# Joining block inverses in four steps in place of nine, in a macaron layer with gated delta-rule attention

## The chip, the core and the metric

The kernel runs on one core of a Trainium2 chip. The metric is the device time of one execution in microseconds (us), the median of several runs. The core has TensorE (PE in the profile; its weight loads are listed apart as PEld), VectorE (DVE), ScalarE (ACT), GpSimd (POOL), and a queue that issues DMA transfers (SP). Each engine works through its own list of instructions in order, and they wait for one another through semaphores.

## What is computed

The input is `x`, 8 batches of 512 rows of 128 numbers, in float32. For each batch:

```python
x = x + 0.5 * ffn(layernorm(x))          # "f1": 128 -> 512 -> 512 -> 512 -> 128, ternary weights
x = x + attn(layernorm(x))               # below
x = x + 0.5 * ffn(layernorm(x))          # "f2", the same weights

def attn(x):                             # 8 heads of 128
    n = layernorm(x) * ln1_w + ln1_b
    q, k, v = l2norm(silu(n @ Wq)), l2norm(silu(n @ Wk)), silu(n @ Wv)
    beta, alpha = sigmoid(n @ Wb), sigmoid(n @ Wa)
    # over time: S = alpha (I - beta k k^T) S + beta v k^T ;  o = S^T q
    x = x + o @ Wo
    return x + gelu(layernorm2(x) @ W1 + b1) @ W2 + b2
```

The recurrence over time is computed in chunks of 128 rows. Within a chunk it needs the inverse of a unit triangular 128x128 matrix for each of 4 chunks x 8 heads = 32 units.

## The kernel before

**The inverse.** Each unit's matrix is cut into blocks of 32. GpSimd inverts the four diagonal blocks of all 32 units together by elimination (`invert`), and DMAs (`back`) put the block inverses into the tile `R` (straight) and their transposed partners into `TB`. TensorE then joins neighbouring blocks, first two of 32 into 64 (for the pair of blocks 0, 1 and the pair 2, 3), then two of 64 into 128. A join is two products: the off-diagonal block times one inverse (kinds `p32` and `p64`; the result goes, negated, to `TB`), then times the other inverse (kinds `r32` and `r64`; the result goes to `R`). For the first pair alone a third product (`t32`) gives the same joined block transposed, which the 64-wide join needs in `TB`. Each matmul is 32x32x32 or 64x64x64 and works on one unit, in the part of the array that its rows and output partitions give.

**The nine steps** (`STEPS`, L272). A step has two sides; side 0 writes bank 6, side 1 bank 7, and the matmuls of the sides alternate: 16 on each side in steps 0 to 4 (32 wide), 8 on each in steps 5 to 8 (64 wide), 224 matmuls in all. A matmul is listed in the trace as two records. After a step VectorE copies bank 6 out (`joined`, L904) and ScalarE bank 7 (L1065), one instruction each, and `join_waits` (L1688) holds TensorE before the next step until both are done. The kinds by step are p32|p32, p32|p32, r32|r32, r32|t32, t32|r32, p64|p64, p64|r64, p64|r64, r64|r64.

**Where the steps run.** The loop over time `t` runs three things of different batches one after the other on TensorE: `SP(t-1, t, t+1)`, the scan over the four chunks of batch s = t-1 mixed with the projections of batch p = t and the start of the first FFN of batch t+1; `F1(t+1)`, the rest of that first FFN; and `F2(t-1)`, the second FFN of batch t-1 in 20 slots. A slot is two matmuls of 512 columns (four records), in the last four slots four matmuls of 128 columns. Steps 0 to 6 of batch t run behind slots 6, 8, 10, 12, 14, 16 and 18 of `F2` (`JOIN_SLOTS`). Steps 7 and 8 (`AHEAD` = 7) run in `SP_first` of the batch, between `solve`, `proj`, `update` and `output`. The last batch has its steps 0 to 6 behind slots 10, 12, 14, 16, 17, 18 and 19 (`LATE_SLOTS`). Batch 0 has no FFN beside it: `lone_join` (L1727) runs steps 0 to 6 one after another, two `proj` between them, with a small matmul (`hold`) ahead of each.

**What stands around the change.** VectorE's order in the second FFN of batch t-1 is joined(t,0), joined(t,1), `LN_F1`, joined(t,2), joined(t,3), then the gates of the next batch with the rest of the copies between. In `SP_first` TensorE's order is solve (two), proj 2 and 3, step 7, update 0, proj 0, update 1, proj 1, output (two), step 8, proj 4 and 5, attend. ScalarE copies the solved rows and the outputs out and applies silu to each projection; a projection's bank (4 or 5) is free again after that silu. VectorE copies the new state, takes `squares` of the keys, and after GpSimd's power normalizes and turns the keys (`unit_k`); then SP stores them (`k_store`) and loads them back turned into `KT` (`k_load`), for `keys_keys(p, 0)` in the next part of the scan.

## Time and profile before

| | us |
|---|---|
| median of 3 runs | 1491.02 |
| lowest and highest | 1490.46, 1491.98 |
| the profiled execution's own time | 1489.32 |
| its span in the trace | 1487.6 |
| TensorE matmul busy | 1418.9 (95%) |
| VectorE, ScalarE, GpSimd busy | 820.9, 668.6, 564.9 |
| mean granted TensorE clock | 0.982 of full |

The steady part repeats with a period of 173.3 us per batch, batches 1 to 6. The rows of the section below are lines of the profile: the busy times, the windows table, the chain that ended last, the timeline of one engine, and the answers for one line of the kernel. In a timeline row the numbers are the start and the duration in us, then the engine, the line, the operation, the result and its inputs, the tile shape, the output shape and the count of records that the row merges; brackets hold the idle time before it and what ended it.

### The profile page before, as it was taken

The page shows a single profiled execution, that of the slowest core. Times are in us where ns is not written, and L with a number is a line of the kernel's source. Part 1 is how long each engine was busy: PE and PEld are TensorE (multiplying, and loading weights), DVE is VectorE, ACT ScalarE, POOL GpSimd, SP SyncE. Part 2 cuts the span into 40 slices and gives each one's busy share as a digit, 9 for nine tenths or more (in the row PEclk, how much of TensorE's full clock was granted, in tenths as well). Part 3 has the DMA queues.
Part 4 walks back from the last instruction along what each step waited for, and adds up shares of the span by engine and source line. Part 5 has one row for each costly group of instructions (what it writes and reads, how often), then busy time and mean ns, then how long its engine had stood idle before and what let it go on. Part 6 is the DMA issues. An engine that isn't in the chain of part 4 may idle for free.

```text
span 1487.6 us, 25821 instructions
## 1 busy us (share of the span) xinstructions
PE 1418.9 (95%) x10118; PEld 966.2 (65%) x10118; DVE 820.9 (55%) x2432; ACT 668.6 (45%) x1130; POOL 564.9 (38%) x641
## 2 busy tenths in 40 slices
PE   7998899999999999999999999999999999889968
PEld 3455776557866587557865588566875578656934
DVE  3467387454865367644764557753776437641330
ACT  2466466225652356325562256523563256512222
POOL 0038042831447133650428314471336504381000
PEclk9999899999999999999999999999999999989979
DMA  5130244532454135630455325641356304543000
GB/s 173 42 100 29 41 104 116 108 82 65 122 115 99 34 88 130 132 82 23 104 123 102 82 65 122 111 106 31 92 126 124 82 23 111 112 77 76 1 0 7
DMA packets 359546, 125.04 MB, mean 84 GB/s; under 512 B 325280, under 2 KB 340352, under 8 KB 359424
## 3 DMA queue, kind: packets, MB, share of 16 engines
q1 hardware_dynamic: 359424, 123.38, 36.2%
q8 instruction: 80, 1.31, 0.3%
q14 instruction: 42, 0.34, 0.1%
HBM read 79.58 MB, written 43.76 MB: 83 GB/s over the span
## 4 chain that ended last, share of the span: by engine, by line
PE 89%; DVE 7%; ACT 1%; DMA 1%; SPq 1%; issue 1%; DVEq 0%; ACTq 0%
PE bank L1284 29%; PE bank L1390 9%; PE bank L1313 5%; PE bank L1292 4%; PE bank L1446 4%; PE bank L1473 4%; PE bank L1482 4%; PE bank L1429 3%; PE bank L1414 3%; PE bank L1454 3%; PE bank L1463 3%; PE bank L1437 3%; PE bank L1706 2%; PE bank L1671 2%; PE bank L1680 2%; PE bank L1715 1%
## 5 line engine op out<-in xcount | busy, mean ns | idle before, releaser
L1284 PE MATMUL bank<-big,h 128*128 128x512 f32 x992 | 447.1, 596 | 0.0
L1284 PEld LDWEIGHTS bank<-big,h 128*128 128x128 f32 x992 | 181.6, 190 | 197.0 <-issue 192.5
L512 POOL TENSOR_TENSOR rnorm<-ssq,mhalf 128x16 f32<-128x16 f32 (+1 forms) x35 | 84.0, 2401 | 516.8 <-DVE ssq L773 516.8
L1390 PE MATMUL bank<-wqkv,nT 128*128 128x512 f32 x336 | 160.2, 596 | 0.0
L558 POOL TENSOR_TENSOR blkT<-blkT,blkP 128x31 f32<-128x31 f32 (+15 forms) x248 | 135.8, 547 | 19.4
L555 POOL TENSOR_TENSOR blkP<-blkA,blkT 128x31 f32<-128x31 f32 (+15 forms) x248 | 129.2, 521 | 31.1 <-DMA blkA<-blocks_out 12.3
L1313 PE MATMUL bank<-xT,w 128*128 128x512 f32 x256 | 122.7, 626 | 8.4 <-ACT xT L1038 4.2
L908 DVE TENSOR_SCALAR TB<-bank 32x512 f32<-32x512 f32 (+1 forms) x48 | 33.1, 689 | 153.0 <-PE bank L1713 74.3
L1055 ACT ACTIVATE big<-bank,cols 128x512 f32<-128x512 f32 x64 | 43.0, 686 | 138.3 <-PE bank L1284 100.4
L887 DVE TENSOR_TENSOR MT<-bank,MT 128x512 f32<-128x512 f32 x56 | 38.6, 691 | 104.3 <-PE bank L1429 104.3
L1313 PEld LDWEIGHTS bank<-xT,w 128*128 128x128 f32 x256 | 49.0, 201 | 66.5 <-issue 50.9
L1062 ACT ACTIVATE big<-bank,cols 128x512 f32<-128x512 f32 x64 | 43.1, 686 | 108.6 <-PE bank L1284 108.5
L521 POOL TENSOR_TENSOR MT<-rows_or_g,maskf 128x1024 f32<-128x1024 f32 x28 | 78.2, 2792 | 11.5 <-PE bank L1473 11.0
L539 POOL TENSOR_TENSOR QET<-QET,sgf 128x1024 f32<-128x1024 f32 x21 | 49.3, 2350 | 86.7 <-DMA sgf<-e_rows 86.7
L1390 PEld LDWEIGHTS bank<-wqkv,nT 128*128 128x128 f32 x336 | 56.8, 191 | 37.4 <-issue 36.8
L1124 ACT ACTIVATE MT<-MT,biasj 128x128 f32<-128x128 f32 x256 | 78.2, 389 | 0.3
L1446 PEld LDWEIGHTS bank<-V,R 128*128 128x128 f32 x512 | 63.0, 196 | 15.0 <-issue 12.5
L1429 PEld LDWEIGHTS bank<-QET,KT 128*128 128x128 f32 x448 | 58.4, 197 | 20.4 <-issue 14.4
L1292 PE MATMUL bank<-w,big 128*128 128x128 f32 x512 | 68.2, 279 | 2.3 <-DVE TB L908 1.5
L1292 PEld LDWEIGHTS bank<-w,big 128*128 128x128 f32 x512 | 62.6, 192 | 11.8 <-issue 8.4
L1134 ACT ACTIVATE big<-bank 128x512 f32<-128x512 f32 x56 | 32.7, 597 | 82.8 <-PE bank L1390 82.7
L1446 PE MATMUL bank<-V,R 128*128 128x128 f32 x512 | 64.7, 281 | 3.7 <-DVE V L915 2.1
(213 smaller groups left out, 2598.6 us busy)
## 6 DMA issues: line engine op xcount, KB each, us to landing
rows_or_g<-g_rows SPq DMA_DIRECT2D x28, 512.0 KB, 4.9
q_rows<-mid SPq DMA_DIRECT2D x28, 512.0 KB, 4.9
QET<-q_rows SPq DMA_DIRECT2D x112, 128.0 KB, 4.2
k_rows<-R SPq DMA_DIRECT2D x27, 512.0 KB, 2.7
KT<-k_rows SPq DMA_DIRECT2D x108, 128.0 KB, 3.6
sgf<-e_rows SPq DMA_DIRECT2D x21, 512.0 KB, 4.6
blocks_out<-R SPq DMA_DIRECT2D x128, 32.0 KB, 1.7
blkA<-blocks_out SPq DMA_DIRECT2D x8, 512.0 KB, 3.8
```

Of the source, the lines that this page charges most:

```text
L512: pool.tensor_tensor(rnorm[:, heads_of], ssq[:, heads_of], mhalf[:, :].to_broadcast([128, heads_of.stop - heads_of.start]), ALU.pow).then_ ...
L521: pool.tensor_tensor(MT[:, u, :], grow, maskf[:, :].unsqueeze(1).to_broadcast([128, H, 128]), ALU.add).then_inc(d_mask, 1)
L555: pool.tensor_tensor(prod, A3[:, j, j + 1:].unsqueeze(2).to_broadcast([128, n, m]), T3[:, j:j + 1, 0:m].to_broadcast([128, n, m]), ALU.mul ...
L558: pool.tensor_tensor(T3[:, j + 1:, 0:m], T3[:, j + 1:, 0:m], prod, ALU.subtract).then_inc(b_prod, 1)
L1124: last = act.activation(MT[:, u, :], MT[:, u, :], ACT.Exp, bias=biasj[:, u:u + 1])
L1284: last = pe.matmul(bank[bk + i][:, :], w[:, k, 128 * o:128 * o + 128], src[:, k, :], start=(k == 0), stop=(k == KB - 1))
L1292: last = pe.matmul(bank[4][:, 128 * c:128 * c + 128], src[:, k, 128 * c:128 * c + 128], w[:, k, :], start=(k == 0 and c == 0), stop=(k == ...
L1313: pe.matmul(bank[bk][:, :], w[:, 128 * o:128 * o + 128], xT[:, :], start=True, stop=True).then_inc(f["gate"], 1)
L1390: pe.matmul(bank[4 + n % 2][:, :], nT[:, 128 * c:128 * c + 128], wqkv[:, i // 2, 512 * (i % 2):512 * (i % 2) + 512], start=True, stop=True ...
L1429: last = pe.matmul(heads(bank[6 + g])[:, h, :], KT[:, u, :], QET[:, u, :], start=True, stop=True)
L1446: last = pe.matmul(heads(bank[g])[:, h, :], R[:, u, :], V[:, u, :], start=True, stop=True)
L1473: last = pe.matmul(heads(bank[2 + g])[:, h, :], V[:, u, :], MT[:, u, :], start=(c == 0 and h == 0), stop=True, skip_group_check=True)
```

## The change

The steps become four, `p32`, `r32`, `p64`, `r64`, each over all 32 units. In step k bank 6 holds units 0 to 15 and bank 7 units 16 to 31. In steps 0 and 1 the matmuls of the two pairs alternate, both into the same bank, at different partitions: 64 matmuls a step. In steps 2 and 3 the units alternate between the output partitions 64 to 127 and 0 to 63 of the same bank, with the same 64 input rows: 32 matmuls a step. The kind `t32` is gone: behind step 1 VectorE copies each bank's result of the first pair to `R` and turns it in 32x32 blocks into `TB`. Both copying engines now follow each bank: VectorE has 2, 4, 2, 2 instructions behind the four steps, ScalarE 2 each. The semaphore counts change with that (`COPIES_DVE`, `COPIES_ACT`). All four steps run in the second FFN, behind slots 6, 9, 12 and 16, for the last batch behind 11, 13, 16 and 18; `SP_first` has none left, and its first solve waits for the first bank of step 3 alone. `keys_keys(b, 0)` waits for both copying engines. `LN_F1` stands behind joined(t,0) in VectorE's queue.

```diff
-JOIN_SLOTS = [6, 8, 10, 12, 14, 16, 18]
-LATE_SLOTS = [10, 12, 14, 16, 17, 18, 19]
+JOIN_SLOTS = [6, 9, 12, 16]
+LATE_SLOTS = [11, 13, 16, 18]
+JOINS = 4
+COPIES_DVE, COPIES_ACT = (0, 2, 6, 8, 10), (0, 2, 4, 6, 8)
...
-        STEPS = [(("p32", (0, 0)), ("p32", (1, 0))), (("p32", (0, 1)), ("p32", (1, 1))),
-                 (("r32", (0, 0)), ("r32", (1, 0))), (("r32", (0, 1)), ("t32", (0, 0))),
-                 (("t32", (0, 1)), ("r32", (1, 1))), (("p64", 0), ("p64", 1)),
-                 (("p64", 2), ("r64", 0)), (("p64", 3), ("r64", 1)), (("r64", 2), ("r64", 3))]
...
+            def joined(b, k):                                   # VectorE
+
+                for x in range(2):
+                    half, first = slice(16 * x, 16 * x + 16), slice(16 * x, 16 * x + 8)
+                    dve.wait_ge(j_full, b * 2 * JOINS + 2 * k + x + 1)
+                    if k == 0:
+                        dve.tensor_scalar(TB[32:64, half, 0:32], units_of(x, 16)[32:64], -1.0, None, ALU.mult).then_inc(j_dve, 1)
+                    if k == 1:
+                        dve.tensor_copy(R[0:32, half, 32:64], units_of(x, 16)[0:32]).then_inc(j_dve, 1)
+                        dve.transpose(TB[32:64, half, 0:32], units_of(x, 16)[0:32]).then_inc(j_dve, 1)
+                    if k == 2:
+                        dve.tensor_scalar(TB[64:128, first, :], units_of(x, 8)[64:128], -1.0, None, ALU.mult).then_inc(j_dve, 1)
+                    if k == 3:
+                        dve.tensor_copy(R[0:64, first, 64:128], units_of(x, 8)[0:64]).then_inc(j_dve, 1)
...
             def SP_first(s, p):
 
-                pe.wait_ge(j_dve, s * NS + AHEAD)
-                pe.wait_ge(j_act, s * NS + AHEAD)
+                pe.wait_ge(j_dve, s * ND + ND - 1)
+                pe.wait_ge(j_act, s * NA + NA - 1)
...
-                join(s, AHEAD, JOIN_BANKS)
                 update(s, 0, 0)
...
-                join_waits(s, AHEAD + 1)
                 output(s, 0, 0), output(s, 0, 1)
-                join(s, AHEAD + 1, JOIN_BANKS)
...
-                if k == 2:
+                if k == 1:
                     pe.wait_ge(b_Rin, b * 4 * 16 + 4 * 16)
...
+            def join(b, k):
+
+                for x in range(2):
+                    for i in range(16):
+                        u = 16 * x + i
+                        if k < 2:
+                            col = slice(32 * i, 32 * i + 32)
+                            for e in (0, 64):
+                                e, o = slice(e, e + 32), slice(e + 32, e + 64)
+                                if k == 0:
+                                    last = pe.matmul(bank[6 + x][o, col], R[e, u, o], TB[e, u, 0:32], start=True, stop=True)
+                                else:
+                                    last = pe.matmul(bank[6 + x][e, col], TB[o, u, 0:32], R[o, u, o], start=True, stop=True)
+                        else:
+                            u = 16 * x + i // 2 + 8 * (i % 2)
+                            col = slice(64 * (i // 2), 64 * (i // 2) + 64)
+                            out = (slice(64, 128), slice(0, 64))[(i + k) % 2]
+                            if k == 2:
+                                last = pe.matmul(bank[6 + x][out, col], R[0:64, u, 64:128], TB[0:64, u, :], start=True, stop=True)
+                            else:
+                                last = pe.matmul(bank[6 + x][out, col], TB[64:128, u, :], R[64:128, u, 64:128], start=True, stop=True)
+                    last.then_inc(j_full, 1)
```

## Rows read from the trace of the kernel before

**Rows 1.** The page's first part: busy us, share of the span, instructions.

```profile
PE 1418.9 (95%) x10118; PEld 966.2 (65%) x10118; DVE 820.9 (55%) x2432; ACT 668.6 (45%) x1130; POOL 564.9 (38%) x641
```

**Rows 2.** Windows table, one batch: length, busy us by engine, clock, DMA share, GB/s.

```profile
322.10:495.40 173.30, 172.61 (x1255) 117.69 (x1254) 103.10 (x303) 81.13 (x135) 73.88 (x81) 1.00 0.41 93
```

**Rows 3.** TensorE's timeline, second FFN, steps 0 and 1 of a batch.

```profile
491.26 1.20 PE L1713 MATMUL bank<-TB,R 32*32 32x32 f32 x64
492.39 3.70 PE L1284 MATMUL bank<-big,h 128*128 128x512 f32 x8
496.03 1.20 PE L1713 MATMUL bank<-TB,R 32*32 32x32 f32 x64
```

**Rows 4.** The chain that ended last, in order of time: start, us, what.

```profile
479.32 12.02 PE bank L1284 x28
...
532.77 2.00 PE bank L1707 x32
```

**Rows 5.** TensorE's timeline, step 3 (r32 beside t32), its first and last record.

```profile
505.99 0.21 PE L1715 MATMUL bank<-R,TB 32*32 32x32 f32 x1
...
507.00 0.19 PE L1716 MATMUL bank<-TB,R 32*32 32x32 f32 x1
```

**Rows 6.** TensorE's timeline, step 6 (p64 beside r64) and the matmul behind it.

```profile
520.46 0.27 PE L1706 MATMUL bank<-TB,R 64*64 64x64 f32 x1
...
520.57 0.22 PE L1706 MATMUL bank<-TB,R 64*64 64x64 f32 x1
...
521.38 0.22 PE L1706 MATMUL bank<-TB,R 64*64 64x64 f32 x1
...
521.54 0.38 PE L1292 MATMUL bank<-w,big 128*128 128x128 f32 x1
```

**Rows 7.** TensorE's timeline, SP_first: proj(p, 0, 0).

```profile
528.21 1.02 PE L1390 MATMUL bank<-wqkv,nT 128*128 128x512 f32 x2
```

**Rows 8.** VectorE's timeline: LN_F1's begin, the copy behind it, a turn of keys.

```profile
497.97 0.87 DVE L620 BATCH_NORM_STATS2 lnf_st<-xin 128x6 f32<-128x128 f32 x4
...
503.09 0.68 DVE L908 TENSOR_SCALAR R<-bank 32x512 f32<-32x512 f32 x1
...
534.30 1.25 DVE L784 STREAM_TRANSPOSE R<-big 128x1024 f32<-128x1024 f32 x1
```

**Rows 9.** The DMAs of line L448 in one batch: issues, and time to landing.

```profile
L448 SPq DMA_DIRECT2D R<-r_back x4: 470/734/873, 479.4 to 481.4; - x4
...
DMA to landing us min/median/max: 3.7/4.1/4.4
```

**Rows 10.** ScalarE's timeline, SP_first: the silus of proj 2 and 3.

```profile
526.52 1.08 ACT L1134 ACTIVATE big<-bank 128x512 f32<-128x512 f32 x2
```

**Rows 11.** Line L372 (k_load), the last issue for chunk 0, batch 5.

```profile
L372 SPq DMA_DIRECT2D KT<-k_rows x1: 1343/1343/1343, 1060.2 to 1060.2; - x1
...
DMA to landing us min/median/max: 4.9/4.9/4.9
```

**Rows 12.** TensorE's timeline: keys_keys(p, 0) of the same batch.

```profile
1067.15 0.39 PE L1414 MATMUL bank<-KT 128*128 128x128 f32 x2
```

**Rows 13.** TensorE's waits, 1340 us to the end: total, times, longest us.

```profile
PE bank L1292 <- DVE TB L908: 1.5, 2, 0.8
...
PE bank L1446 <- DVE TB L908: 0.8, 1, 0.8
PE bank L1292 <- DVE R L908: 0.8, 1, 0.8
```

**Rows 14.** Windows table, a stretch of batch 0's joins; the clock is third from last.

```profile
165.00:167.00 2.00, 1.20 (x30) 1.08 (x25) 0.68 (x1) 0.59 (x1) 0.00 (x0) 0.50 0.00 0
```

**Rows 15.** TensorE's timeline: batch 0's first join step and its first update.

```profile
154.76 1.20 PE L1713 MATMUL bank<-TB,R 32*32 32x32 f32 x64
...
179.23 1.94 PE L1454 MATMUL bank<-V,KD 128*128 128x128 f32 x15
```

**Rows 16.** TensorE's waits, 170 to 250 us.

```profile
PE bank L1414 <- DMA KT<-k_rows: 1.5, 1, 1.5
```

More of the change, by code:

```diff
@@ L49 @@
 NG = NC + 1
-JOIN_BANKS = (6, 7)
 def place(b, c, i):
@@ L268, in build_program, with units_of @@
         m_xab, m_xab2, m_x2 = sem("m_xab"), sem("m_xab2"), sem("m_x2")
-        STEPS = [(("p32", (0, 0)), ("p32", (1, 0))), (("p32", (0, 1)), ("p32", (1, 1))),
[3 rows of a table removed]
-        NS = len(STEPS)
-        AHEAD = NS - 2
-        def join_result(k, side, banks):
-            kind, part = STEPS[k][side]
-            bk = bank[banks[side]]
-            if kind in ("p64", "r64"):
-                u = slice(8 * part, 8 * part + 8)
-                src = bk[:, :].rearrange("p (u n) -> p u n", u=8)
-                return (src[64:128], TB[64:128, u, :], -1.0) if kind == "p64" else (src[0:64], R[0:64, u, 64:128], 1.0)
-            pair, half = part
-            u = slice(16 * half, 16 * half + 16)
-            e, o = slice(64 * pair, 64 * pair + 32), slice(64 * pair + 32, 64 * pair + 64)
-            src = bk[:, :].rearrange("p (u n) -> p u n", u=16)
-            if kind == "p32":
-                return src[o], TB[o, u, 0:32], -1.0
-            return (src[o], TB[o, u, 0:32], 1.0) if kind == "t32" else (src[e], R[e, u, o], 1.0)
+        ND, NA = COPIES_DVE[JOINS], COPIES_ACT[JOINS]
+        def units_of(x, n):
+            return bank[6 + x][:, :].rearrange("p (u n) -> p u n", u=n)
         block = ctx.enter_context(nc.Block())
@@ L1002, in _ @@
             gates_abs(1), gates_log(1), cumulated(1)
-            for k in range(AHEAD):
+            for k in range(JOINS):
                 joined(0, k)
@@ L1014, in _ @@
             gating("f2", B - 3, 2), gating("f2", B - 3, 3), N(B - 1)
-            for k in range(4):
+            for k in range(3):
                 joined(B - 2, k)
-            gates_abs(B - 1), joined(B - 2, 4), gates_log(B - 1), joined(B - 2, 5), cumulated(B - 1), joined(B - 2, 6)
+            gates_abs(B - 1), gates_log(B - 1), joined(B - 2, 3), cumulated(B - 1)
             result("f2", B - 3, x2)
@@ L1024, in _ @@
                 decayed_q(B - 1, c, 0), decayed_q(B - 1, c, 1)
-            for k in range(AHEAD):
+            for k in range(JOINS):
                 joined(B - 1, k)
@@ L1207, in P_alone @@
                 N_logs(1), silu(1, 0, 2), silu(1, 0, 3), joined(0, 0), silu(1, 0, 0), joined(0, 1), silu(1, 0, 1)
-                for k in range(2, AHEAD):
-                    joined(0, k)
+                joined(0, 2), joined(0, 3)
             def SP_first(s, p):
@@ L1410, in keys_keys @@
                 else:
-                    pe.wait_ge((j_dve, j_act)[g], b * NS)
+                    pe.wait_ge(j_dve, b * ND)
+                    pe.wait_ge(j_act, b * NA)
                 for h in range(4):
@@ L1662, in P_alone @@
                 lone_join(0), proj(1, 0, 0), lone_join(1), proj(1, 0, 1)
-                for k in range(2, AHEAD):
-                    lone_join(k)
+                lone_join(2), lone_join(3)
             def M_up(b, f1):
@@ L1691, in join_waits @@
                     pe.wait_ge(p_dq, b * 2 * NC + 2 * NC)
-                if k == 2:
+                if k == 1:
                     pe.wait_ge(b_Rin, b * 4 * 16 + 4 * 16)
                 if k > 0:
-                    pe.wait_ge(j_dve, b * NS + k)
-                    pe.wait_ge(j_act, b * NS + k)
-            def join_one(k, side, i, banks):
-                kind, part = STEPS[k][side]
-                bk = bank[banks[side]]
-                if kind in ("p64", "r64"):
-                    u = 8 * part + i
-                    col = slice(64 * i, 64 * i + 64)
-                    if kind == "p64":
-                        return pe.matmul(bk[64:128, col], R[0:64, u, 64:128], TB[0:64, u, :], start=True, stop=True)
-                    return pe.matmul(bk[0:64, col], TB[64:128, u, :], R[64:128, u, 64:128], start=True, stop=True)
-                pair, half = part
-                e, o = slice(64 * pair, 64 * pair + 32), slice(64 * pair + 32, 64 * pair + 64)
-                u = 16 * half + i
-                col = slice(32 * i, 32 * i + 32)
-                if kind == "p32":
-                    return pe.matmul(bk[o, col], R[e, u, o], TB[e, u, 0:32], start=True, stop=True)
-                if kind == "r32":
-                    return pe.matmul(bk[e, col], TB[o, u, 0:32], R[o, u, o], start=True, stop=True)
-                return pe.matmul(bk[o, col], R[o, u, o], TB[o, u, 0:32], start=True, stop=True)
```

49 lines of the change are left out of this document (23 added, 26 removed).

## The prediction

> **What bounds the kernel now.** I read the page's busy times first, then the windows table for a whole batch, then the timelines of each engine around the join steps. TensorE is busy for 1418.9 of 1487.6 us [rows 1]. A window of one batch gives it 172.61 of 173.30 us at full granted clock, while VectorE has 103, ScalarE 81 and GpSimd 74 us [rows 2]; a window laid over the next batch reads the same. So in batches 1 to 6 the period is TensorE's own work: what leaves its queue leaves the time, unless the removed work covered something. Only the first 180 us, the last batch's joins and the tail are different.
>
> **What one join costs TensorE now.** A 32-wide step is 32 matmuls, each two records. Its 64 records begin at 491.26, the next 512-column record at 492.39, the next join at 496.03: 4.77 us for a join and eight records of 512 columns [rows 3]. Such a record costs 12.02/28 = 0.429 us [rows 4], so the join costs 4.77 - 3.43 = 1.34 us. Its records start 0.0159 us apart (505.99 to 507.00 over 63) [rows 5], which is 1.02 us; the other 0.32 us are the change into small tiles and back, paid once per join. A 64-wide step whose two sides differ in rows and columns of the array (kinds p64 and r64) starts 32 records in pairs, 0.058 us per pair (520.57 to 521.38 over 14), and takes 1.08 us to the next matmul (520.46 to 521.54) [rows 6]. One whose sides use the same tile (two p64 or two r64) takes 2.00 us [rows 4], 0.117 us for what is a pair there. With the 0.21 us that the 32-wide steps lose around these figures (1.34 - 1.13), they are 1.29 and 2.21 us.
> Before, a batch pays 5 x 1.34 + 2 x 2.21 + 2 x 1.29 = 13.7 us, of which 10.2 in the second FFN and 3.5 in SP_first.
>
> **After.** Steps 0 and 1 are 64 matmuls (128 records): 128 x 0.0159 + 0.32 = 2.36 us each. The 32 matmuls of kind t32 (64 records, 1.02 us) are gone, done by VectorE's block turn. Steps 2 and 3 are 32 matmuls that alternate between two column halves on the same 64 rows, in one bank. No step of before has this at 64 columns. The bounds are the 0.058 us per pair of the mixed step and the 2 x 0.058 us of the same-tile step, so 1.87 or 3.74 us for 64 records, plus 0.34. I take the lower, because step 3 of before (L1715 beside L1716, both on rows 32 to 63, columns 0 to 31 against 32 to 63) runs at 0.0159 us a record, no slower than a step on different rows (64 records, 1.13 us) [rows 3, 5]. That is 2.21 us each. A batch pays 2 x 2.36 + 2 x 2.21 = 9.1 us: 4.6 less (0.8 if the upper bound holds). Of it 10.2 - 9.1 = 1.1 is in the second FFN and 3.5 in SP_first.
> The Trainium skill (TensorE: Matmul & The Clock Gate, Part 3, The mechanism) says that a weight load overlaps with running matmuls only when its row group differs. By that rule steps 2 and 3 would not overlap, as in the first rival; step 3 of before speaks against it.
>
> **What the removed work covered.** Second FFN: joined(k) now has two copies on each engine, and step 1 two copies and two turns on VectorE. A copy takes 0.68 us from PSUM; the one transpose in the trace takes 1.25 us for 128x1024, so 0.65 us for 512 elements a row, from half of that to twice it as bounds [rows 8]. The first bank's are done beside the second half of the step, so 0.1 + 0.69 us are left behind steps 0, 2, 3, and some 1.5 (3 at the upper bound) behind step 1. Between a step and the wait for it lie two slots (3.4 us) or three: hidden, at nothing, and at up to 0.7 us a step without that cover. LN_F1 stands in VectorE's queue before joined(t,1): it takes 5.1 us (497.97 to 503.09, when the next copy begins) [rows 8] and has some 5.5 us before the first half of step 1 is done; at worst 0.5 us late, still before the wait. R is loaded by 481.4 + 4.4 = 485.8 [rows 9], and slot 9 comes after the first join at 491.26 [rows 3]: the earlier wait for b_Rin is free.
> SP_first: two things come nearer. (a) proj(p,0,0) waits for silu(p,0,2) (bank 4). ScalarE does the two copies of solved, a table load, then the silus from 526.52; the first of the two ends about 527.13 [rows 10]. TensorE would be there at 528.21 - 1.29 = 526.92 [rows 7]: 0.25 us of stall a batch. (b) keys_keys(p,0) waits for KT: update, state copy, squares, power, unit_k, k_store, k_load. Of six batches the worst has its last load issued at 1060.2, landed 4.9 us later (1065.1), used at 1067.15 [rows 11, 12]: 2.05 us of slack. TensorE comes 3.5 - 0.25 = 3.25 us earlier; the chain starts at update(s,0,0) and comes 1.2 us earlier, so the slack falls to 0.0 in that batch and stays above it elsewhere. I book 0.3 us in all.
> Queues: PE's waits on j_dve and j_act are earlier satisfied than before; VectorE has one instruction more a batch, ScalarE one less, and no DMA is added or moved. exps on ScalarE no longer stands behind a join of slot 18.
>
> **The sum**, against the profiled run (span 1487.6, its own time 1489.3 us):
> - Second FFN, batches 1 to 6: 6 x 1.1 = 6.4 us.
> - SP_first, s = 1 to 6: 6 x (3.5 - 0.25) - 0.3 = 19.2 us.
> - The last batch's joins (F2_late) have slots of 0.9 us between them and wait for copies: four stalls, 3.1 us [rows 13]. After, slot 17 lies behind step 2 and slot 19 behind step 3, whose first half suffices to begin. 3.1 + 1.1 = 4.2 us.
> - SP_first, s = 7: nothing beside it, TensorE bound: 3.5 us.
> - Start: from the first join record (154.76) to update(0,0,0) (179.23) 24.5 us [rows 15]; in it TensorE stands some 0.8 us behind each lone join, and the granted clock is at half (1.2 GHz) in the window from 165 to 167 [rows 14]; the update's records are at full pace again. With four steps: at full clock throughout, 2.2 + 0.9 + 0.3 + 2.2 + 1.9 + 0.3 + 2.0 + 1.1 + 2.0 (the first half's copy beside it) + 0.2 + 1.8 = 14.7 us, 9.8 less; with steps 2, 3 and the solve at half clock, 1.8 + 1.8 + 1.8 more, 4.4 less. I take 7. After this the first SP waits 1.5 us on KT already [rows 16], so its second removed join only lengthens that wait: 0.
> Sum 40 us: 1489.3 - 40 = 1449. The median of the runs is 1.7 us above the profiled one: 1451 us, with 1446 to 1460 for this case (start 4.4 to 9.8, cover lost, small errors).
>
> **Rivals.**
> 1. Column halves on the same rows don't overlap at 64 columns. For: no row of before shows that pairing at this width. Against: step 3 of before, which has it at 32 columns at full rate [rows 5]. Price: 1.87 x 2 x 8 = 30 us, 1481 us: still faster.
> 2. Slower than before: two tiles writing one bank take turns. Before, the alternating sides always wrote banks 6 and 7; after, both write bank 6 + x in all four steps. The trace has no such pair. If they take turns, steps 0 and 1 cost 2.04 us more each, 2 and 3 1.87: 7.8 x 8 = 63 us, 1514 us. It decides once more than 5.0 of these 7.8 us a batch are lost. Against it: the outputs are in different partitions, and every other four-matmul group fills one bank without a gap. The Trainium skill (TensorEngine Tiling (Array Packing), Gotcha 1) says that different row tiles can't access one bank at once; steps 0 and 1 do that, and by the rule alone they would take turns.
> 3. The cover is thinner than I think: the KT chain doesn't move up (3 us in all), and 128 records in a row can't be issued at 0.0159 us. In the lone joins 64 records follow 0.3 us of the holding matmul, so the supply may be as slow as 1.3/64 = 0.020 us: 0.5 x 2 x 8 = 8 us. Together 1462 us.
>
> **How the numbers follow.** Forecast 0.68, rival 3 0.12, rival 1 0.12, rival 2 0.05, below 1446 0.03. The range 1446 to 1473 takes in the forecast, rival 3 and a part of a lost overlap, and leaves out rivals 1 and 2 and the low tail. 0.2% (3 us) is what a measurement can tell: all of the forecast, rivals 3 and 1 are faster; same is a part-way rival 2.
>
> **What would show it.** Records 0.016 us apart in steps 0 and 1, pairs 0.058 us apart in steps 2 and 3, where 0.117 would be rival 1 and 0.032 us a record rival 2; a batch period of 173.3 - 4.3 = 169.0 us; a wait of about 0.25 us of proj on silu (L1134's copy out of bank 4) in each SP_first; keys_keys without a wait on KT but in the first SP; no stall in the last batch's joins; a granted clock that falls later or not at all between 160 and 175 us. The prediction is wrong if the period stays above 171 us.

## The result and the profile after

The changed kernel takes 1454.26 us (median of 4 runs, 1452.58 to 1454.58). The kernel before took 1491.5 us in the same series (4 runs, 1490.46 to 1496.28). The ratio is 0.9742, with a 95% interval of 0.972 to 0.9764: 2.6% faster. The forecast was 1451 us.

The profiled execution of after took 1452.58 us, its span is 1450.9 us and its mean granted clock 0.978. Before it was 1489.32, 1487.6 and 0.982. So 36.7 us of span are to be found. The busy times of after, the page's first part (answers to [rows 1]):

```profile
PE 1386.9 (96%) x9600; PEld 943.4 (65%) x9600; DVE 832.8 (57%) x2440; ACT 666.4 (46%) x1122; POOL 565.0 (39%) x641
```

TensorE is busy 32.0 us less and still for 96% of the span. It remains the bound.

The chain of work that ended last has one row that recurs in every batch, 28 records of 512 columns just ahead of the joins. Its starts cut the run into batches (start, length, what; in after the row of the second batch is missing from the chain and stands in the timeline at 471.11):

```profile
302.19 12.02 PE bank L1283 x28
641.53 12.02 PE bank L1283 x28
810.63 12.02 PE bank L1283 x28
979.72 12.02 PE bank L1283 x28
1148.91 12.02 PE bank L1283 x28
```

Before, the marks stand at 306.00, 479.32 [rows 4], 652.65, 825.97, 999.30 and 1172.63. Three sums follow.
- **Up to the first mark**: 306.00 to 302.19, 3.8 us less.
- **Five periods**: 1172.63 - 306.00 = 866.6 us before and 1148.91 - 302.19 = 846.7 us after, 19.9 us less. The period was 173.33 us and is 169.09 us, except for the one from 471.27 to 641.53, which has 170.26.
- **Behind the last mark**: 1487.6 - 1172.63 = 315.0 us before and 1450.9 - 1148.91 = 302.0 us after, 13.0 us less.

Now one batch of after in TensorE's timeline (start, length, line, output<-inputs, tile, shape, count; answers to [rows 3, 5, 6]):

```profile
483.22 2.21 PE L1704 MATMUL bank<-TB,R 32*32 32x32 f32 x128
485.37 5.42 PE L1283 MATMUL bank<-big,h 128*128 128x512 f32 x12
490.71 2.21 PE L1706 MATMUL bank<-R,TB 32*32 32x32 f32 x128
492.86 3.70 PE L1283 MATMUL bank<-big,h 128*128 128x512 f32 x8
...
498.64 2.08 PE L1712 MATMUL bank<-TB,R 64*64 64x64 f32 x64
500.66 1.98 PE L1283 MATMUL bank<-big,h 128*128 128x512 f32 x4
...
507.79 2.08 PE L1714 MATMUL bank<-R,TB 64*64 64x64 f32 x64
509.80 1.16 PE L1291 MATMUL bank<-w,big 128*128 128x128 f32 x8
```

From the start of a step to the start of the next matmul it is 2.15, 2.15, 2.02 and 2.01 us. No row carries an idle time in brackets, so no step waited. (A PE row's length is modelled at its end, so the steps are timed from start to start.) By the method of [rows 3], the first join and the twelve records behind it take 490.71 - 483.22 = 7.49 us, less 12 x 0.429 = 5.15: 2.34 us for the join with all that it costs around it.

TensorE's waits in 430 to 600 us (what waited <- for whom: total, times, longest):

```profile
PE bank L1414 <- DMA KT<-k_rows: 0.9, 1, 0.9
PE bank L1312 <- DVE big L658: 0.7, 1, 0.7
```

and in the stretch of the first scan, 150 to 260 us (answers to [rows 16]):

```profile
PE bank L1446 <- DVE V L908: 2.4, 1, 2.4
PE bank L1414 <- DMA KT<-k_rows: 0.6, 1, 0.6
```

The first list holds the one longer period: a wait for KT. The second holds the first scan, to which the experiments come.

The joins of batch 0, alone, with work of TensorE between them (timeline, the wait in brackets; answers to [rows 15]):

```profile
153.13 2.55 PE L1704 MATMUL bank<-TB,R 32*32 32x32 f32 x128
155.62 2.08 PE L1389 MATMUL bank<-wqkv,nT 128*128 128x512 f32 x2
...
157.84 3.62 PE L1706 MATMUL bank<-R,TB 32*32 32x32 f32 x128
...
163.61 3.68 PE L1712 MATMUL bank<-TB,R 64*64 64x64 f32 x64
168.08 0.58 PE L1682 MATMUL bank<-ident 128*128 128x1 f32 x2 [0.80 <-DVE TB L899]
168.60 3.68 PE L1714 MATMUL bank<-R,TB 64*64 64x64 f32 x64
172.21 3.47 PE L1446 MATMUL bank<-V,R 128*128 128x128 f32 x16
175.52 2.01 PE L1454 MATMUL bank<-V,KD 128*128 128x128 f32 x16
```

Steps 1 to 3 take 3.6 us here against the 2.0 to 2.2 us of the steady batch, and two records of 512 columns take 1.9 us where they take 0.9. The windows table says why (window, its length, then busy us and counts by engine; the third number from the end is the granted clock; answers to [rows 14]):

```profile
150.00:155.00 5.00, 4.06 (x121) 2.98 (x121) 1.61 (x7) 4.49 (x6) 0.00 (x0) 0.97 0.92 111
155.00:160.00 5.00, 5.00 (x112) 3.89 (x110) 0.95 (x3) 1.39 (x3) 0.00 (x0) 0.50 0.27 105
...
170.00:175.00 5.00, 5.00 (x57) 4.88 (x54) 2.54 (x6) 1.79 (x3) 0.00 (x0) 0.50 0.01 2
175.00:180.00 5.00, 5.00 (x39) 4.53 (x39) 3.29 (x13) 1.79 (x3) 0.44 (x1) 0.98 0.00 0
```

The clock is at half (1.2 GHz) from about 154.7 us, inside the first join step (0.97 in 150 to 155), to about 175. In the profile of before it was full until 164.

### The profile page after: what moved, and what is told of

It reads as the page before. It is cut to its first block, busy times and chain, and to the rows that moved or that the text cites. A ratio compares the mean times of both kernels' runs of the same rounds, so it can differ in the third digit from the quotient of the medians.

```text
span 1450.9 us, 24752 instructions
## 1 busy us (share of the span) xinstructions
PE 1386.9 (96%) x9600; PEld 943.4 (65%) x9600; DVE 832.8 (57%) x2440; ACT 666.4 (46%) x1122; POOL 565.0 (39%) x641
## 4 chain that ended last, share of the span: by engine, by line
PE 81%; DVE 7%; issue 5%; POOL 3%; ACT 2%; DMA 1%; SPq 0%; DVEq 0%; POOLq 0%; ACTq 0%
PE bank L1283 26%; PE bank L1389 9%; PE bank L1312 5%; PE bank L1446 4%; PE bank L1291 4%; PE bank L1473 4%; PE bank L1482 4%; PE bank L1414 3%; PE bank L1429 3%; PE bank L1463 3%; PE bank L1454 3%; PE bank L1437 3%; PE bank L1667 2%; PE bank L1676 2%; POOL blkT L542 1%
## 5 line engine op out<-in xcount | busy, mean ns | idle before, releaser
L1312 PE MATMUL bank<-xT,w 128*128 128x512 f32 x256 | 119.7, 613 | 8.8 <-DVE big L658 4.6
L1446 PEld LDWEIGHTS bank<-V,R 128*128 128x128 f32 x512 | 64.4, 200 | 14.7 <-issue 10.1
L1482 PEld LDWEIGHTS bank<-wo,blkA 128*128 128x128 f32 x512 | 61.3, 192 | 10.0 <-issue 10.0
```

Of the source, the lines that this page charges most:

```text
L1312: pe.matmul(bank[bk][:, :], w[:, 128 * o:128 * o + 128], xT[:, :], start=True, stop=True).then_inc(f["gate"], 1)
L1446: last = pe.matmul(heads(bank[g])[:, h, :], R[:, u, :], V[:, u, :], start=True, stop=True)
L1482: last = pe.matmul(bank[2][:, 0:D], oT[:, hh, :], wo[:, hh, :], start=(hh == 0), stop=(hh == H - 1))
```

## The experiments

Theory: (T1) what a step costs is its records in sequence, and the two halves of the array and the two column halves overlap when their matmuls alternate, whatever bank they write; (T2) each visit to small tiles costs some 0.3 us apart from its records; (T3) the start gained little because of the clock and of a chain on VectorE. The rivals are in the expectations. Each kernel was compared with the kernel before on the same chip.

### Do the overlaps that the sum rests on exist?

**Column halves in runs.** Steps 2 and 3 of after, with the eight matmuls of one column half of a bank first, then those of the other.

```diff
-                            u = 16 * x + i // 2 + 8 * (i % 2)
-                            col = slice(64 * (i // 2), 64 * (i // 2) + 64)
-                            out = (slice(64, 128), slice(0, 64))[(i + k) % 2]
+                            col = slice(64 * (i % 8), 64 * (i % 8) + 64)
+                            out = (slice(64, 128), slice(0, 64))[(i // 8 + k) % 2]
```

> The changed kernel, but in steps 2 and 3 the eight matmuls of one column half run together and then the eight of the other, in place of taking turns; same matmuls, same banks, same copies. My theory (two column halves on the same 64 rows overlap when they alternate): each of these steps goes from 2.02 us to about 3.9 us, +1.87 us x 2 steps x 7 batches, and twice that in batch 0 at half clock, about +33 us: 1487 us, and pairs of records 0.117 us apart. Rival (the gain comes from fewer steps alone, the order within a step does nothing): no change, 1454 us.

Measured: 1477.31 us (1476.99 to 1479.27), ratio 0.9892 [0.9872, 0.9911], 23 us above after. Step 2 in its timeline:

```profile
507.94 3.40 PE L1711 MATMUL bank<-TB,R 64*64 64x64 f32 x64
511.28 1.98 PE L1283 MATMUL bank<-big,h 128*128 128x512 f32 x4
```

It takes 3.34 us to the next matmul where the alternating one takes 2.02. The period is 171.72 us (825.24 to 996.96 in its chain), 2.63 us = 2 x 1.32 above after. So the overlap of alternating column halves on the same rows is real. Its size was expected at 1.87 us a step and is 1.32. The joins of batches 1 to 7 and those of batch 0, at half clock, account for it: 7 x 2.63 = 18.4 us, and from the first join to the first update it takes 27.1 us (154.00 to 181.11) against 22.4, 4.7 more; together 23.1.

**Pairs in runs.** Steps 0 and 1 of after, 16 matmuls of the upper half of the array into a bank, then 16 of the lower half.

```diff
-                    for i in range(16):
+                    for n in range(32 if k < 2 else 16):
+                        i = n % 16
...
-                            for e in (0, 64):
+                            for e in (64 * (n // 16),):
```

> The changed kernel, but in steps 0 and 1 the 16 matmuls of the first pair of blocks run together and then the 16 of the second, bank by bank. My theory (the two pairs overlap although both write one bank): each step goes from 2.15 us to at most 4.2 us, so up to +2.04 x 2 x 7 + 8 in batch 0, between +15 and +37 us: 1469 to 1491 us. Rival (issue sets the 0.016 us a record, or two tiles writing one bank take turns already): no change, 1454 us.

Measured: 1508.85 us (1496.61 to 1513.11, 10 runs), ratio 1.0102 [1.0073, 1.0131]: 1% slower than before, and outside what was expected. The two steps in TensorE's timeline:

```profile
495.39 3.93 PE L1705 MATMUL bank<-TB,R 32*32 32x32 f32 x128
504.60 4.13 PE L1707 MATMUL bank<-R,TB 32*32 32x32 f32 x128
```

and the windows over the end of the second and behind it (0.81 and 0.92 are the clock; ahead of it, 500 to 505 us, it is 1.00):

```profile
505.00:510.00 5.00, 5.00 (x123) 4.42 (x121) 2.74 (x5) 1.18 (x2) 0.00 (x0) 0.81 0.02 3
510.00:520.00 10.00, 10.00 (x87) 5.46 (x86) 1.57 (x3) 4.50 (x6) 0.00 (x0) 0.92 0.01 2
```

The records alone cost 3.9 to 4.1 us a step instead of 2.2, so in after the two row halves overlap inside one bank. The second rival (turns at the bank) is false: with turns, alternating would cost what the runs cost. The rest of the loss was not foreseen. Its last three periods are 175.9, 177.4 and 177.7 us, more than the 169.09 + 4 of the records. The granted clock falls to half at the end of the long step and stays there for some 3 us, although the profile counts TensorE busy in every microsecond (5.00 of 5.00, clock 0.81); the eight records of 512 columns behind the step take 4.95 us (508.66 to 513.61) and not 3.54 as in after (492.86 to 496.40). Mean clocks of its runs are 0.956 to 0.970; the fastest has the highest.

**Two halves of the array in before.** Before alone has steps 5 and 8 with both sides on one tile [rows 4]. Here their second side is put on the other half.

```diff
+                if side == 1 and k == 5:
+                    return src[0:64], TB[64:128, u, :], -1.0
+                if side == 1 and k == 8:
+                    return src[64:128], R[0:64, u, 64:128], 1.0
...
+                    if side == 1 and k == 5:
+                        return pe.matmul(bk[0:64, col], R[0:64, u, 64:128], TB[0:64, u, :], start=True, stop=True)
+                    if side == 1 and k == 8:
+                        return pe.matmul(bk[64:128, col], TB[64:128, u, :], R[64:128, u, 64:128], start=True, stop=True)
```

> The kernel before with its nine steps; only in steps 5 and 8, whose two sides used the same tile of the array, side 1 now writes the other 64 partitions of bank 7, so that the sides differ in columns and share the rows. My theory: each of the two steps goes from 2.00 to 1.08 us, -0.92 x 2 x 8 = -14.7 us, less about 1 us of new stalls: 1477 us. Rival (a pair on the same rows doesn't overlap at 64 columns unless something else of the change is there): no change, 1491 us.

Measured: 1476.66 us (1475.31 to 1478.06), ratio 0.9885 [0.9864, 0.9905]. The period is 171.47 us (304.10, 475.57, 647.04, 818.50 in its chain), 1.86 below before. Nine steps kept, it has 15 of the 37 us: the pairing alone brings these, here with the two sides in different banks.

### What a visit and the moved turn are worth

**The turn back on TensorE.** After, with the 32 matmuls of kind t32, which make the transposed block of the first pair, returned to step 1, and a plain copy on VectorE.

```diff
-                        dve.transpose(TB[32:64, half, 0:32], units_of(x, 16)[0:32]).then_inc(j_dve, 1)
+                        dve.tensor_copy(TB[32:64, half, 0:32], units_of(x, 16)[32:64]).then_inc(j_dve, 1)
...
+                                    if e.start == 0:
+                                        pe.matmul(bank[6 + x][o, col], R[o, u, o], TB[o, u, 0:32], start=True, stop=True)
```

> The changed kernel, but the transposed block of the first pair comes from 32 matmuls in step 1 again (96 matmuls in the step), and VectorE copies it straight in place of the block turn. My theory: step 1 goes from 2.15 to 3.17 us, +1.02 x 7 + 2 in batch 0 at half clock = +9 us: 1463 us. Rival (the additional tile runs in the shadow of the two others, or the time goes where VectorE's turn was): no change, 1454 us.

Measured: 1468.62 us (1464.66 to 1471.75, 4 runs), ratio 0.9829 [0.9803, 0.9855], 14 us above after where 9 were expected. The step itself speaks against the expectation. One of them in TensorE's timeline, its first record and what follows:

```profile
1008.10 0.21 PE L1707 MATMUL bank<-TB,R 32*32 32x32 f32 x1
...
1010.25 3.70 PE L1283 MATMUL bank<-big,h 128*128 128x512 f32 x8
```

The 96 matmuls, 192 records, take 2.15 us to the next matmul, as the 64 matmuls of after do, and not 3.17. The third tile ran in the shadow of the two others, as the rival had it, at 0.011 us a record: that records cost their time in sequence (T1) holds for two alternating tiles, not for three. The loss lies beside the records. In five of the seven steps of batches 1 to 7 TensorE stops in the step or just behind it, and the profile names no engine and no DMA that it waits for ("issue"): 1.6, 1.5, 1.5, 1.1 and 2.3 us. One of them:

```profile
499.64 0.21 PE L1708 MATMUL bank<-R,TB 32*32 32x32 f32 x2 [1.54 <-issue]
```

After has no such wait. Behind the first of the five (327.03) the granted clock is at half too, 0.50 from 328 to 330 us. Together that is 8.0 us of standing and 1.6 of half clock, in a span that is 12.0 us longer. Its periods, 172.53, 170.86, 170.84, 170.31 and 169.94 us, fall with these waits; that the last two lie 0.9 to 1.2 us above after, near the 1.0 us of 64 records, is chance (a stop of 1.1 us in one, a wait of 0.6 us for KT in the other). Why TensorE stops there was not tried. Its executions of 1469.61 and 1471.75 us have mean granted clocks of 0.971 and 0.972, the other two 0.976 and 0.977; neither of the two slower ones was profiled. So this run shows that the version with the turn on VectorE is the quicker one, and does not show a price of 1 us for the 64 records. VectorE's two turns cost 0.71 us each (0.65 was estimated) and nobody waits for them. The groups of after by form (count | busy us, mean ns | idle before, and for whom):

```profile
L897 DVE STREAM_TRANSPOSE TB<-bank 32x512 f32<-32x512 f32 x16 | 11.3, 706 | 0.5
L896 DVE COPY R<-bank 32x512 f32<-32x512 f32 x16 | 10.9, 679 | 14.5 <-PE bank L1706 14.1
```

**Eight visits for four.** After, with each step of batches 1 to 6 cut at its two banks and put behind two slots. The records are the same.

```diff
-                        join(b + 1, join_slots.index(s))
+                        join(b + 1, join_slots.index(s), (0,) if started else (0, 1))
+                    if started and s - 1 in join_slots:
+                        join(b + 1, join_slots.index(s - 1), (1,))
...
-            def join(b, k):
-
-                for x in range(2):
+            def join(b, k, banks=(0, 1)):
+
+                for x in banks:
```

> The changed kernel, but for batches 1 to 6 each step is cut at its two banks: bank 6's half runs behind its slot and bank 7's half behind the next slot. Same matmuls and copies, eight visits to the small tiles in place of four. My theory (a visit costs 0.32 us besides its records): +0.32 x 4 x 6 = +7.7 us, 1462 us. Rival (the saving comes from the matmuls alone, a visit is free): no change, 1454 us.

Measured: 1461.38 us (1460.66 to 1461.83), ratio 0.9796 [0.9778, 0.9814], 7.1 us above after and 6.1 above the unchanged after on the same chip (1455.32, below) for 24 more visits: 0.25 to 0.3 us each. Its last three periods are 170.39 to 170.67 us (645.65, 816.04, 986.61, 1157.28), 1.3 to 1.6 above after for four visits. So five visits fewer are worth 1.3 to 1.5 us a batch with no record removed. With the 1.86 us of the pairing, an estimate of 0.9 to 1.1 of the 4.24 us a batch is left for the 64 records of t32, which took time of their own in before, where only two tiles alternate in a step.

### How near is the KT chain?

**Before and after with eight bn_stats (1.6 us of VectorE) ahead of unit_k(p, 0).** In before the slack of 2.05 us should take the delay; in after it should show.

```diff
                 if p is not None:
+                    for i in range(H, 2 * H):
+                        dve.bn_stats(bst[:, i, :], triu[:, :])
                     unit_k(p, 0)
```

> The kernel before with 1.6 us of unneeded work on VectorE (eight bn_stats of a constant) ahead of unit_k of chunk 0, in the chain that ends in the load of KT. It leaves nothing out. My theory (in batches 1 to 6 the load had at least 2.05 us of slack): only the first scan, which waits on KT already, and the seventh batch's get longer: +1.6 to +2 us, 1493 us. Rival (KT is late in every batch): +11 us, 1502 us.

> The changed kernel with the same 1.6 us on VectorE ahead of unit_k of chunk 0. My theory (the removed joins were the cover: 0 to 1.1 us of slack are left): a wait on KT of 0.5 to 1.6 us in each of batches 2 to 7 and more in the first, +6 to +10 us, 1460 to 1464 us. Rival (the slack is as large as before): +2 us, 1456 us.

Measured: before delayed 1493.67 us (12 runs), ratio 1.0008 [0.9995, 1.0021], period 173.33 us as ever. After delayed 1458.31 us (1454.89 to 1459.67), ratio 0.9772 [0.9752, 0.9793]: 3 to 4 us above after and not the 6 to 10 expected; three of its five periods are 169.09, the others 170.68 and 169.44. The miss is in the placing. In after VectorE stands idle just there, for GpSimd's power. Its timeline in after:

```profile
520.87 0.68 DVE L916 COPY state<-bank 128x512 f32<-128x512 f32 x1
522.71 1.23 DVE L762 TENSOR_TENSOR big<-big,rnorm 128x1024 f32<-128x1024 f32 x1 [1.16 <-POOL rnorm L496]
```

From the copy's start to the normalizing it is 1.84 us in after and 2.15 us (524.37 to 526.52) with the eight instructions between. The delay that reached the chain there was 0.3 us. It is the same in before: 1.84 us (531.20 to 533.04) without and 2.15 (536.50 to 538.65) with the eight instructions. So before delayed says nothing on a slack of 2.05 us; that figure rests on [rows 11, 12] alone. The first scan has LN_F1 in front of the eight, no idle time takes them up, and they show whole, as a wait for V: 4.0 us in after delayed against 2.4, 2.5 in before delayed against 1.0.

**The delay behind the wait.** The same eight instructions behind the normalizing of chunk 0, ahead of its turn, where nothing hides them. The squares of the next chunk, which write to the same scratch `bst`, wait for that turn.

```diff
+                if g == 1:
+                    dve.wait_ge(k_turned, (b - 1) * NC + 1)
...
+                if c == 0:
+                    for i in range(H, 2 * H):
+                        dve.bn_stats(bst[:, i, :], triu[:, :])
                 dve.wait_ge(p_unit, b * NC + c + 1)
```

> The changed kernel with eight unneeded bn_stats (1.63 us) between the normalizing and the turn of unit_k for chunk 0, where VectorE has no idle time in front of them as it had in the run before (there 1.16 us of the 1.6 fell into its wait for GpSimd's power). My theory (0.5 to 1.0 us of slack on KT are left in five batches, none in the third): waits of 0.6 to 1.1 us in five batches, 1.6 in one, 1.6 in the first scan: +8 us over the changed kernel, 1463 us. Rival (there is slack of 2 us as before the change): +1.6 us, 1457 us.

Measured: 1460.58 us (1460.0 to 1465.88), ratio 0.9797 [0.9768, 0.9826], between the two. TensorE now waits for KT in each of batches 2 to 7. Its waits in 430 to 1280 us (total, times, longest):

```profile
PE bank L1419 <- DMA KT<-k_rows: 5.4, 5, 1.8
```

By batch the six waits are 0.3, 1.1, 0.7, 0.8, 1.0 and 1.8 us. From the normalizing to the turn it is 2.69 us (525.28 to 527.97) against 1.26 in after (522.71 to 523.97), so the chain was held up by 1.43 us. Less the waits that leaves slacks of 1.1, 0.3, 0.7, 0.6, 0.4 and -0.4 us. The first scan doesn't wait for KT at all; there the delay goes into the wait for V (3.9 us against 2.4). So after the change the chain ends some 0.3 to 1.1 us ahead of its use, and a transfer that takes longer eats it. That is the wait of 0.9 us in one batch of after: SP issued the store of k_rows there at 525.24 and the first load at 529.75, 4.5 us later, against 2.6 us (695.49 to 698.10) a batch on.

### The start

**After once more**, unchanged, for how the start differs from one execution to the next.

> The changed kernel unchanged, as the measure for its variants on this chip: 1454 us. Of interest is also the stretch of batch 0's joins: whether the granted clock falls to half at the same place as in the first profile (155 us), and whether a wait on KT of about 1 us shows in one of the later batches again or in another.

Measured: 1455.32 us (1453.73 to 1458.75), ratio 0.976 [0.974, 0.978]. Its first join begins at 154.07 us, its first update comes 22.4 us later as in the first profile, the clock is again at half from about 156 to 176, and the scan waits 2.4 us for V. It waits for KT twice, 0.4 us each, in 430 to 600 and in 940 to 1110 us, besides the 0.6 us of the first scan: which batch is late changes.

**Filled gaps.** After, with TensorE kept busy around the lone joins: two matmuls of 512 columns into an unused bank ahead of N_sums(1), one ahead of each of steps 1 to 3. Their output is never read.

```diff
-                proj(1, 0, 2), proj(1, 0, 3), N_sums(1)
+                proj(1, 0, 2), proj(1, 0, 3)
+                for _ in range(2):
+                    pe.matmul(bank[3][:, :], ident[:, :], nT[:, :], start=True, stop=True)
+                N_sums(1)
...
             def lone_join(k):
+                if k > 0:
+                    pe.matmul(bank[3][:, :], ident[:, :], nT[:, :], start=True, stop=True)
```

> The changed kernel with matmuls that nothing needs in batch 0's lone joins: two of 512 columns ahead of N_sums and one ahead of the wait of steps 1 to 3, into bank 3. My theory (the granted clock falls there because TensorE stands between the steps): the clock stays at 2.4 GHz, steps 1 to 3 and the first solve take half their time, -6 us, and the fillers cost 1: 1450 us. Rival (the clock falls on the small matmuls themselves, however full the queue is): the clock falls as before and the fillers cost 2 to 4 us: 1458 us.

Measured: 1447.08 us (1446.25 to 1448.9), ratio 0.9702 [0.9675, 0.9729], mean clocks 0.983 to 0.986. The joins of batch 0 in TensorE's timeline:

```profile
154.79 2.21 PE L1707 MATMUL bank<-TB,R 32*32 32x32 f32 x128
...
158.96 2.21 PE L1709 MATMUL bank<-R,TB 32*32 32x32 f32 x128
...
163.44 2.08 PE L1715 MATMUL bank<-TB,R 64*64 64x64 f32 x64
...
166.63 2.08 PE L1717 MATMUL bank<-R,TB 64*64 64x64 f32 x64
168.64 2.05 PE L1446 MATMUL bank<-V,R 128*128 128x128 f32 x16
170.53 2.01 PE L1454 MATMUL bank<-V,KD 128*128 128x128 f32 x16
```

and its windows:

```profile
155.00:160.00 5.00, 5.00 (x199) 3.99 (x192) 1.65 (x4) 1.87 (x4) 0.00 (x0) 1.00 0.30 111
160.00:165.00 5.00, 4.96 (x133) 3.60 (x128) 3.13 (x5) 2.13 (x4) 0.00 (x0) 1.00 0.02 3
```

With more work on TensorE the stretch from the first join to the first update is 15.7 us instead of 22.4, because every step runs at full clock (2.4 GHz). The wait for V in the first scan stays (2.5 us), and so does the half clock behind it.

**LN_F1 out of the first scan.** After, with the second row block's LN_F1, which VectorE does inside the first scan, cut in three and put between the copies of the lone joins.

```diff
-                if p == 1:
-                    LN_F1(2)
...
-            for k in range(JOINS):
-                joined(0, k)
+            joined(0, 0)
+            dve.wait_ge(ld_x, 3 * 16)
+            moments(ln_f["f1"], 2, xin)
+            joined(0, 1), inverse(ln_f["f1"], 2), joined(0, 2), normed(ln_f["f1"], 2, xin, xin), joined(0, 3)
```

> The changed kernel with LN_F1(2) taken from the first scan's VectorE queue, ahead of unit_k, into batch 0's lone joins, cut in three between the copies. My theory (the second removed join was worth nothing in the first scan, since VectorE's chain sets its waits: 2.4 us on V, 0.6 us on KT, and the half clock after them): those waits go, 3 to 5 us less: 1450 us. Rival (the copies of the lone joins get later by what LN_F1 takes, and the gain is given back): 1455 us.

Measured: 1449.04 us (1445.05 to 1450.59), ratio 0.9707 [0.9678, 0.9736]. The second solve in TensorE's timeline, first that of after:

```profile
188.75 3.68 PE L1446 MATMUL bank<-V,R 128*128 128x128 f32 x16 [2.43 <-DVE V L908]
192.25 1.97 PE L1463 MATMUL bank<-QET,state 128*128 128x128 f32 x16
```

and then with LN_F1 moved:

```profile
187.68 1.95 PE L1446 MATMUL bank<-V,R 128*128 128x128 f32 x16
189.47 1.95 PE L1463 MATMUL bank<-QET,state 128*128 128x128 f32 x16
```

The wait is gone, and with it the half clock of the 16 records behind it (3.50 us from one row to the next in after, 1.79 here). From the first update to that solve it is 10.6 us instead of 13.2. That is 2.6 us, and the span of the profiled execution is 3.1 us shorter than the control's (1448.9 and 1452.0, the control being the unchanged after above), while the medians differ by 6.3. The profiled execution is the slowest of the five (1450.59 us, mean clock 0.978, with the early half clock in its lone joins); the three quickest (1445.05 to 1449.04) have 0.982 to 0.985, which no execution of after has. So a part of the 6.3 us is likely the clock in the lone joins; it was not profiled.

**Both.** The two edits together, the version that should beat both kernels.

> The changed kernel with both edits at once: the second row block's LN_F1 is cut in three and put between the copies of the lone joins of the first batch, and the filler matmuls of 512 columns stand in the gaps of those joins. Each edit alone gave about 5 to 7 us. If the two gains are separate (one ends VectorE's lateness in the first scan, the other keeps the clock at 2.4 GHz during the lone joins) they add: about 1441 us. The rival is that both save the same stretch at half clock, or that the LN_F1 pieces lengthen the gaps that the fillers had shortened: about 1446 us, no better than the better of the two alone by more than 1 us.

Measured: 1444.21 us (1442.55 to 1448.93), ratio 0.9681 [0.9659, 0.9703]. It stands between the two expected figures, 2.9 us under the filled one and 11.1 under the control (1455.32), where the single gains were 8.2 and 6.3. In its profile both effects are whole: 16.1 us from the first join to the first update (158.63 to 174.69) and 10.6 us from there to the second solve (185.33), without a wait. (That profile is of the slowest of the five executions, 4.7 us above the median; its first join begins some 4 us later than in the other profiles.) Two things can hold back the missing 3.4 us, and the runs don't part them. One is the expectation's rival: if half of the 6.3 us was the clock in the lone joins, as above, the fillers bring that part already, and it counts once: 8.2 + 3.1 = 11.3 would be the whole sum. The other is the KT chain, whose slack is spent. Its timeline here:

```profile
192.43 2.05 PE L1414 MATMUL bank<-KT 128*128 128x128 f32 x16 [1.58 <-DMA KT<-k_rows]
```

1.6 us of wait in the first scan against 0.6 in after, 0.4 in the filled one and 0.7 with LN_F1 moved, and 1.3 us in the next batch, against none, 0.2 and none.

## Why the prediction was right, point by point

- **The bound.** TensorE bound before and after; its period gave all of the steady gain.
- **What a step costs.** Predicted 2.36 us for each 32-wide one and 2.21 for each 64-wide one, measured 2.34 for the first by the same method, and 2.15 and 2.02 us from the first record to the next matmul, where the prediction has 2.15 and 2.00 without the 0.21 us around a step. The period was predicted at 169.0 us and is 169.09. One reading of the term is too strong: 0.0159 us a record is the pace of two alternating tiles and not of records as such, since with three tiles 192 records take the same 2.15 us.
- **The lower bound for column halves.** It was taken from the 32-wide step 3 of before and it held: the halves in runs show what is lost without it. There the upper bound was mis-sized: 1.32 us a step, not 1.87. Within a run the records keep the slow pace (15 begin in the first 0.80 us of the step), but the last record of one half and the first of the other still overlap in part (six begin in the next 0.20 us). The first rival would have cost 8 x 2.6 = 21 us, not 30. The Trainium skill's rule (TensorE: Matmul & The Clock Gate, Part 3, The mechanism), that a weight load overlaps only where the row group differs, isn't what these rows show: steps 2 and 3 use the same 64 rows throughout and run 64 records in 2.02 us, and 3.34 when they don't alternate.
- **Two tiles in one bank.** The second rival fell: steps 0 and 1 put two row tiles into one bank in 2.15 us for 128 records and need 3.9 to 4.1 in runs. The Trainium skill (TensorEngine Tiling (Array Packing), Gotcha 1) says that different row tiles can't access one bank at the same time. The trace doesn't agree, at least where they write different partitions of it.
- **The cover.** Nothing in the second FFN waits for a copy or a turn in after. The stall of proj(p, 0, 0) on silu was predicted at 0.25 us; it begins at 518.03 where it would have been due at 517.88, so 0.15.
- **KT.** Predicted slack 0.0 in the worst batch, measured waits of 0.9 us (first profile) and 0.4 and 0.4 (the control), slacks of 0.3 to 1.1 in most others. 0.3 us was booked; about 1 is paid. The sign "keys_keys without a wait on KT but in the first SP" failed. The third rival was partly real: the chain is what the next gain would hit, as the last experiment shows. Its other half, records that can't be issued at 0.016 us, was not.
- **The sum.** Five periods: predicted 5 x (1.1 + 3.25) - 0.3 = 21.4, measured 19.9 (5 x 4.24 = 21.2, less 1.3 in the batch that waited for KT). Behind the last mark: predicted 1.1 + 3.25 + 4.2 + 3.5 = 12.05, measured 13.0; the last batch's joins have no stall left, and TensorE's waits from 1280 to 1415 us name none of their copies. The 0.95 us beyond the sum were not traced. Two slips of the sum weigh nothing: 6 x 1.1 is 6.6 and not 6.4, and the eleven terms of the start at full clock add up to 14.9 and not 14.7.
- **The start is the term that was mis-sized.** 7 us were booked, 3.8 measured, and even of these 1.6 lie ahead of the first join (154.76 and 153.13), where both kernels do the same work and where profiles of after and its variants differ by more (153.13 to 154.86, and 158.63 in one). From the first join to the first update it is 24.5 us [rows 15] and 22.4, 2.1 less. The step that failed is the clock's course: half clock was supposed for steps 2, 3 and the solve at worst, as in the profile of before, and it began inside step 0, at about 154.7 us. (The prediction's TensorE that stands 0.8 us behind each lone join is true of five of the seven: the two with a proj behind them have no idle time.) An early fall needs no change: the delayed kernel before, whose joins are untouched, has it at the same point, as its windows show:

```profile
154.00:156.00 2.00, 2.00 (x38) 1.08 (x32) 0.68 (x1) 0.73 (x2) 0.00 (x0) 0.73 0.76 88
156.00:158.00 2.00, 2.00 (x67) 1.99 (x65) 0.00 (x0) 0.60 (x1) 0.00 (x0) 0.50 0.26 55
```

Its stretch from the first join to the first update takes 29.5 us (153.33 to 182.82). Like against like, four steps save 7.1 us there. The profiled execution of before had the late fall. The 50 executions of before in the four later series fit this: 21 have a mean granted clock of 0.980 or more and a median of 1489.3 us (1487.3 to 1493.0), 29 have less and 1494.3 us (1490.9 to 1500.7). All nine executions of after have 0.975 to 0.979. So in before both courses are common and in after only the early one was seen; whether the four longer steps make it more frequent is open, as mean clocks of two kernels don't compare strictly. The full-clock sum of 14.7 us was near what the filled gaps gave, 15.7 with three fillers inside the stretch.
- **The second removed join of the first scan** was booked at nothing, because of KT. It did bring nothing, but most of it went into another wait: V on VectorE, 1.0 us before and 2.4 after, with half clock behind it; KT went from 1.5 [rows 16] to 0.6. VectorE's LN_F1 in that scan was the cause, as the moved LN_F1 shows.

Why the clock falls early in one execution and late in another stays open. The filled gaps show that records ahead of and between the same four steps can keep it from falling; what tips the balance in before was not tried.

## What to carry to other kernels

When many small matmuls share the array, let them alternate between tiles in issue order, in rows or in columns, and into one bank at different partitions if that is easier: runs on one tile cost 3.3 to 4.1 us where alternating ones cost 2.0 to 2.2. Merge visits to small tiles, since each costs 0.25 to 0.3 us beside its records; but a visit of 96 matmuls, three tiles wide, took 2.15 us for its records and stood up to 2.3 us more, so look at the waits of a longer one. And read a stretch's granted clock in several executions before a gain there is priced: a stretch at half clock can be cured by filler work more cheaply than by removing steps (8 us for five filler matmuls, 2 to 7 for five steps).

## What the runs showed of the hardware

- The granted clock fell to 1.2 GHz while TensorE was busy without a gap, at the end of and behind a step of 32x32 records in runs (0.81 in 505 to 510 us of the pairs in runs).
- Five matmul instructions of 512 columns ahead of and between the same joins kept it at 2.4 GHz in both profiles that had them.
- Two row tiles, or two column halves on the same rows, overlap inside one bank: 128 records of 32x32 in 2.15 us, 64 records of 64x64 in 2.02. Three tiles of 32x32 alternating took 2.15 us for 192 records, but TensorE then stopped for 1.1 to 2.3 us in five of seven such steps.
- A block turn of 32x512 from PSUM on VectorE took 0.71 us, as long as a plain copy (0.68).
